# Edge loop of a graph network: the one register load per turn on TensorE moved from the twelfth step to the sixth

## The chip, the core and the metric

The kernel runs on one core of one Trainium2 chip. The metric is the device time of one execution in microseconds, the median over several runs.

## What is computed

Three message-passing layers over a graph with 3125 nodes, 100,000 edges taken in both directions, 128 node features and 16 edge features, then a residual and a layer norm. The core of the reference:

```python
for l in range(3):
    e_in = concat([h_prev[s2], h_prev[d2], ef2])          # gather two nodes per edge
    msg  = leaky_relu(e_in @ We1[l]) @ We2[l]
    red  = segment_sum(msg, d2, num_segments=N)           # scatter-add to nodes
    out  = leaky_relu(concat([h_prev, red]) @ Wn1[l]) @ Wn2[l]
    h_prev = out + h_prev
return layernorm(x + out)
```

## The kernel before

A preparation phase (up to about 1670 us) sorts the edges by the pair of node blocks that they join, so that a tile of 128 edges touches one low and one high block of 128 nodes. In each layer TensorE first multiplies the nodes by the weights (tables t_hi and t_lo, a high and a low half in float16), and then runs the edge loop over all tiles.

The edge loop is a hardware loop with 26 turns in each of the three layers, 78 in all. A turn is unrolled into 12 steps (STEPS = 12; the texts number them q = 0 to 11), a step takes three tiles (STEP = 3). On TensorE one step is, in program order:

- tile 0: `features` (L1089, a matmul into the sums bank, gath6) and four gathers (L1096) that pick table rows by a one-hot matrix gsel;
- tile 1: the same into gath, after a wait for x_set;
- tile 2: the same into gath, with a wait for mlo_set ahead of the gathers;
- sums: 12 matmuls (L1151) that add the messages of three steps ago (LAG = 3) to the node sums, after a wait for gath6_free.

ScalarE copies the gathered values out of the two PSUM places, clears the one in sums (L591) and makes a float16 copy (L597); VectorE applies the leaky ReLU (L806) and makes the low half (L875). In layer 0 VectorE also builds the one-hot matrices (L892 and L810), which are kept in HBM for layers 1 and 2.

Which blocks a tile touches is known at run time only. Each step has one 32-bit word that holds the six block numbers of its three tiles. The words lie in the SBUF row map_row, and TensorE's sequencer loads 15 of them (WORDS = STEPS + LAG: the 12 of the turn and the 3 before it, for the sums) into registers with one TENSOR_LOAD per turn, in `load_words` (L1038). `places` (its register work is put down to L1069 for the gathers and to L1077 for the sums) takes the fields out of a word. A field that was already taken out of the same copy of the words is reused: at steps 3 to 11 the sums of step q use fields that the gathers of step q - 3 took out in the same turn; at steps 0 to 2 they have to be taken out anew, from the words of the turn before. The register work appears in listings of the program as ISA rows and in the trace as FUSED_REGOPS on TensorE's sequencer; the engine named PEldq is that sequencer.

Of the kernel before, what the change touches and what calls it, by code (L numbers as in the profile page):

```python
# [32 lines left out]
STEPS = 12  # L33
LAG = 3
# [26 lines left out]
BANKS = -(-NODES // BANK)  # L61
AHEAD = 1
WORDS = STEPS + LAG
BLOCK_BITS = 5
assert NB <= 1 << BLOCK_BITS and STEP * 2 * BLOCK_BITS < 32
SLOPE = 0.01
# [14 lines left out]
def build(nc, x, src, dst, ef, We1, We2, Wn1, Wn2, c_iota, c_part, c_tri, c_ident, c_tiles, c_steps, c_mask, out):  # L81
# [9 lines left out]
    with ExitStack() as ctx:  # L91
        def sb(name, shape, dt):
            return ctx.enter_context(nc.sbuf_tensor(name, shape, dt))
# [76 lines left out]
        map_row = sb("map_row", [1, MAP_ROW], I32)  # L170
# [158 lines left out]
        def live_counts(engine):  # L329

            _, v = nc.values_load_multi_w_load_instructions(
                map_row[0:1, MAPW * P:MAPW * P + 2], engines=(engine,), min_val=1, max_val=TURNS,
                skip_runtime_bounds_check_because="counted among the turns and batches; the first always counts")
            return v
# [4 lines left out]
        def upto(p):  # L339

            return DMA * (p // 2 + 1)
# [278 lines left out]
        def _(dve):  # L620
            steps = [0]

            def then(ins):

                steps[0] += 1
                ins.then_inc(dve_seq, 1)
                dve.wait_ge(dve_seq, steps[0])
# [141 lines left out]
            for i in range(STEP):  # L769
                for s in range(2):  # L770
                    up = (2 * i + s) * BLOCK_BITS - 7
                    then(dve.tensor_scalar(tile_i[:, :, i, s], tile_i[:, :, i, s], abs(up), None,
# [170 lines left out]
        def _(pe):  # L943
# [43 lines left out]
            live_n, live_p = live_counts(mybir.EngineType.PE)  # L987
            words = [pe.alloc_register(f"word_{k}") for k in range(WORDS)]

# [22 lines left out]
            with pe.Fori(0, L) as l:  # L1012
# [23 lines left out]
                def load_words(first):  # L1036

                    pe.reg_load(words, map_row[0:1, ds(first, WORDS)])  # L1038

                load_words(0)  # L1040
                with nc.Fori(0, TURNS, engines=(mybir.EngineType.PE,), hint_back_edge=True) as it:
                    with pe.If(it < live_n):
                        word_of = [pe.snap(r) for r in words]
                        step0 = pe.snap(l * live_n * STEPS + it * STEPS)
                        turn = pe.snap((l * live_n + it) * PER_TURN)

                        def places(t):

                            q, i = divmod(t, STEP)
                            word, nodes = word_of[q + LAG], []  # L1050
                            for k in (2 * i, 2 * i + 1):
                                field = word // (1 << k * BLOCK_BITS) if k else word
                                if k + 1 < 2 * STEP:
                                    field = field - word // (1 << (k + 1) * BLOCK_BITS) * (1 << BLOCK_BITS)
                                nodes.append(nc.s_assert_within(
                                    field * P, 0, (NB - 1) * P,
                                    skip_runtime_bounds_check_because="a word holds the blocks of three tiles"))
                            return nodes

                        def rows(t, node0, plane):  # L1060

                            return t[:, plane * NODES:(plane + 2) * NODES].rearrange("p (k n) -> p k n", k=2)[:, :, ds(node0, P)]

                        def gather_rows(t):

                            lo, hi = places(t)
                            at = rows(t_hi, lo, 0), rows(t_lo, lo, 0), rows(t_hi, hi, 1), rows(t_lo, hi, 1)
                            for ap in at:
                                pe.lower_ap(ap)  # L1069
                            return at  # L1070

                        def sum_places(t):

                            lo, hi = places(t)
                            at = sums[:, ds(lo, P)], sums[:, ds(hi, P)]
                            for ap in at:
                                pe.lower_ap(ap)  # L1077
                            return at

                        def at_least(value):  # L1080

                            v = pe.snap(value)
                            pe.lower_val(v)
                            return v

                        def features(uv, t, h, fresh):

                            tc = t % PART
                            pe.matmul(uv, fchunk[:, h, tc * P:(tc + 1) * P], wst[:, :, :].rearrange("p s f -> p (s f)"),  # L1089
                                      start=fresh, stop=False, skip_group_check=True)  # L1090

                        def gather(uv, at, t, h, n):

                            tc = t % PART
                            s = n // 2
                            return pe.matmul(uv, gsel[:, h, (2 * tc + s) * P:(2 * tc + s + 1) * P], at[n], start=False,  # L1096
                                             stop=n == 3, skip_group_check=True)

                        for q in range(STEPS):
                            p = q // PART_STEPS  # L1100
                            h = p % 2
                            t = STEP * q
                            first = q % PART_STEPS == 0
                            uv6, uv7 = gath6, (gath[:, 0:2 * D], gath[:, 2 * D:4 * D])


                            rows0 = gather_rows(t)
                            if first:
                                part_in = at_least(turn + upto(p))
                            x_free = at_least(step0 + (q + AHEAD))  # L1110
                            if first:
                                pe.wait_ge(fchunk_in[h], part_in)
                            features(uv6, t, h, False)
                            if first:
                                pe.wait_ge(gsel_set[h], part_in)
                            for n in range(4):
                                last = gather(uv6, rows0, t, h, n)
                            last.then_inc(gath6_done, 1)


                            rows1 = gather_rows(t + 1)
                            pe.wait_ge(x_set, x_free)
                            features(uv7[0], t + 1, h, True)
                            for n in range(4):
                                gather(uv7[0], rows1, t + 1, h, n)


                            rows2 = gather_rows(t + 2)
                            free6 = at_least(step0 + (q + 1))
                            lo_in = at_least(step0 + (q + LO_AHEAD - LAG + 2))  # L1130
                            if first:
                                pe.wait_ge(ssel_set[1 - h], part_in)
                            features(uv7[1], t + 2, h, True)
                            pe.wait_ge(mlo_set, lo_in)
                            for n in range(4):
                                last = gather(uv7[1], rows2, t + 2, h, n)
                            last.then_inc(gath7_done, 1)


                            place = (q - LAG) % RING  # L1140
                            sum_at = {t + i - STEP * LAG: sum_places(t + i - STEP * LAG) for i in range(STEP)}
                            if q == STEPS - 1:
                                load_words((it + 1) * STEPS)
                            pe.wait_ge(gath6_free, free6)
                            for i in range(STEP):
                                at_lo, at_hi = sum_at[t + i - STEP * LAG]
                                ts = (t + i - STEP * LAG) % SLOTS
                                for s, out_n in ((1, at_hi), (0, at_lo)):
                                    w0 = i * 2 * D + (1 - s) * D
                                    for m in (m_hi, m_lo):  # L1150
                                        last = pe.matmul(out_n, m[:, place, w0:w0 + D], ssel[:, ts, s, :], start=False,  # L1151
                                                         stop=False, skip_group_check=True)
                            last.then_inc(sum_done, 1)
# [69 lines left out]
```

## Time and profile before

| what | value |
|---|---|
| median of 3 runs | 4555.39 us (4554.65 to 4555.74) |
| the profiled execution's own time | 4540.66 us |
| its span, first to last instruction | 4538.9 us |
| TensorE matmul busy | 3134.0 us, 69% |
| VectorE busy | 2927.2 us, 64% |
| ScalarE busy | 2092.5 us, 46% |
| TensorE's granted clock, mean over the span | 0.806 |

The shares are means over stages with different limits; the change concerns the edge loop alone, which fills three stretches of the span. "Idle before" is time in which an engine had nothing to run, with the releaser that ended it; "issue" as a releaser means that nothing in the trace was being waited for, so that the engine's own sequencer had not yet handed the instruction over.

### The profile page before, as it was taken

How to read it: one execution, taken by the hardware profiler on the slowest of the kernel's cores; microseconds unless marked ns; L12 is line 12 of the kernel's file. 1: busy time of each engine (PE TensorE's matmuls, PEld its weight loads, DVE VectorE, ACT ScalarE, POOL GpSimd, SP SyncE). 2: the span in 40 equal slices, each digit the busy share in tenths (PEclk: the TensorE clock that was granted, in tenths of full speed). 3: DMA queues.
4: the chain of work that ended last, by engine and by line, in shares of the span. 5: the costliest groups of instructions: out<-in, count | busy, mean ns of one | idle time of the engine just before them, and what ended most of it. 6: DMA issues, size and time to landing. Idle time of an engine off the chain costs nothing.

```text
span 4538.9 us, 95215 instructions
## 1 busy us (share of the span) xinstructions
PE 3134.0 (69%) x28957; PEld 2255.1 (50%) x28958; DVE 2927.2 (64%) x7075; ACT 2092.5 (46%) x4052; POOL 780.5 (17%) x826
## 2 busy tenths in 40 slices
PE   3443443443442558888888879898888788988886
PEld 2111111111110556666666657777777577767774
DVE  7444444444443369999999966666666566666665
ACT  0000000000000346666666667777777677777774
POOL 0455555555555100000000000000000000000000
PEclk6555555555555779999999989999999899999998
DMA  6000000000000646666565624444444244444443
GB/s 176 4 5 5 5 5 5 5 5 5 5 5 5 147 123 212 207 213 209 207 215 204 214 102 162 162 154 163 153 159 157 86 164 152 164 152 159 157 155 112
DMA packets 191495, 533.07 MB, mean 117 GB/s; under 512 B 34359, under 2 KB 71958, under 8 KB 189430
## 3 DMA queue, kind: packets, MB, share of 16 engines
q1 hardware_dynamic: 163926, 517.51, 34.1%
q0 software_dynamic: 27552, 15.37, 1.8%
q8 instruction: 6, 0.10, 0.0%
q14 instruction: 11, 0.09, 0.0%
HBM read 375.40 MB, written 157.52 MB: 117 GB/s over the span
## 4 chain that ended last, share of the span: by engine, by line
PE 46%; DVE 10%; issue 9%; DMA 2%; ACT 1%; POOL 0%; DVEq 0%; SPq 0%; ACTq 0%; POOLq 0%
PE gath L1096 16%; PE sums L1151 12%; PE sums L1096 8%; PE gath L1089 5%; DVE loop_buf L875 3%; DVE loop_buf L892 2%; DVE big L806 2%; PE sums L1089 2%; DMA recc<-records 2%; PE sums L1001 1%; DVE gsel L810 1%; PE sums L1159 0%; PE sums L1021 0%; PE sums L1160 0%; PE sums L1165 0%
## 5 line engine op out<-in xcount | busy, mean ns | idle before, releaser
L806 DVE SCALAR_TENSOR_TENSOR big<-big 128x768 f32<-128x768 f32 (+1 forms) x957 | 907.7, 949 | 676.4 <-ACT big L593 635.0
L1096 PE MATMUL gath<-t_hi,gsel 128*128 x3744 | 944.9, 278 | 0.0
L1096 PE MATMUL gath<-t_lo,gsel 128*128 x3744 | 944.3, 278 | 0.0
L1151 PE MATMUL sums<-loop_buf 128*128 128x128 f16 x11232 | 793.7, 221 | 202.6 <-issue 202.0
L875 DVE TENSOR_TENSOR loop_buf<-big,loop_buf 128x768 f16<-128x768 f32 x936 | 889.7, 951 | 0.0
L507 POOL DMA_INDIRECT records<-rec,rowi x784 | 754.7, 963 | 630.7 <-DVE rec L747 391.2
L984 PE MATMUL sums<-t_lo,tri 128*128 128x326 f16 x784 | 345.5, 454 | 714.0 <-issue 480.2
L1151 PEld LDWEIGHTS sums<-loop_buf 128*128 128x128 f16 x11232 | 680.7, 99 | 311.0 <-issue 156.8
L725 DVE SCALAR_TENSOR_TENSOR gsel<-sums,t_lo 128x326 f32<-128x326 f32 x784 | 367.3, 496 | 724.0 <-remote 536.6
L597 ACT ACTIVATE loop_buf<-big 128x768 f16<-128x768 f32 x936 | 782.0, 836 | 1.9
L593 ACT ACTIVATE big<-gath 128x512 f32<-128x512 f32 x936 | 559.6, 598 | 356.8 <-PE gath L1096 356.8
L545 ACT ACTIVATE rec<-big,sc_ef 128x224 f16 x56 | 27.0, 482 | 1356.0 <-DMA records<-rec,rowi 1239.2
L984 PEld LDWEIGHTS sums<-t_lo,tri 128*128 128x128 f16 x784 | 81.8, 104 | 1068.0 <-issue 598.4
L588 ACT ACTIVATE big<-sums 128x256 f32<-128x256 f32 x936 | 355.4, 380 | 422.8 <-PE sums L1096 421.1
L1089 PE MATMUL gath<-wst,fchunk 128*128 128x256 f16 x1872 | 527.1, 282 | 0.6
L1096 PE MATMUL sums<-t_hi,gsel 128*128 x1872 | 468.7, 277 | 22.9 <-DVE gsel L810 22.9
L1096 PE MATMUL sums<-t_lo,gsel 128*128 x1872 | 469.4, 277 | 0.0
L1096 PEld LDWEIGHTS gath<-t_lo,gsel 128*128 128x128 f16 x3744 | 374.1, 100 | 50.6
L1096 PEld LDWEIGHTS gath<-t_hi,gsel 128*128 128x128 f16 x3744 | 374.5, 100 | 31.3
L1089 PE MATMUL sums<-wst,fchunk 128*128 128x256 f16 x936 | 259.6, 277 | 171.2 <-issue 141.0
L591 ACT ACTIVATE sums<-iota 128x256 f32<-128x256 f16 x936 | 362.9, 388 | 29.6
L527 POOL PARTITION_ALL_REDUCE mxa<-mx x3 | 1.1, 358 | 1961.0 <-DVE mx L827 1961.0
(156 smaller groups left out, 2632.1 us busy)
## 6 DMA issues: line engine op xcount, KB each, us to landing
gsel<-gsel_d SPq DMA_DIRECT2D x208, 576.0 KB, 3.9
loop_buf<-ssel_d SPq DMA_DIRECT2D x208, 576.0 KB, 5.1
numb<-nums_d SPq DMA_DIRECT2D x106, 576.0 KB, 4.6
gsel_d<-gsel SPq DMA_DIRECT2D x104, 576.0 KB, 5.5
ssel_d<-loop_buf SPq DMA_DIRECT2D x104, 576.0 KB, 6.5
fchunk<-feat_d SPq DMA_DIRECT2D x313, 144.0 KB, 2.9
records<-rec,rowi POOLq DMA_INDIRECT x784
recc<-records POOLq DMA_DIRECT2D x30, 272.0 KB, 5.1
```

The costliest lines, as they stand in the source:

```text
L507: pool.indirect_dma_start(out=records[:, :], out_offset=bass.IndirectOffsetOnAxis(ap=rowi[:, h, g:g + 1].bitcast(U32), axis=0), in_=rec[:, ...
L588: act.activation(msg[:, place, 0:2 * D], gath6, ACT.Copy).then_inc(x6_set, 1)
L591: act.activation(gath6, iota[:, 0:2 * D], ACT.Copy, scale=0.0).then_inc(gath6_free, 1)
L593: act.activation(msg[:, place, 2 * D:MSG], gath[:, :], ACT.Copy).then_inc(x_set, 1)
L597: act.activation(m_hi[:, (q - 1) % RING, :], msg[:, (q - 1) % RING, :], ACT.Copy)\
L725: dve.scalar_tensor_tensor(scrap[c], bank(1 + c)[:, 0:BUCKETS], 1.0, onehot[:, c * GROUP + g, :], ALU.mult, ALU.mult, accum_out=slot_f[:, ...
L806: return dve.scalar_tensor_tensor(m, m, SLOPE, m, ALU.mult, ALU.max)
L875: dve.tensor_tensor(m_lo[:, place, :], msg[:, place, :], m_hi[:, place, :], ALU.subtract)\
L984: pe.matmul(bank(1 + c)[:, 0:BUCKETS], tri[:, 1, :], onehot[:, c * GROUP + g, :], start=False, stop=False, skip_group_check=True)
L1089: pe.matmul(uv, fchunk[:, h, tc * P:(tc + 1) * P], wst[:, :, :].rearrange("p s f -> p (s f)"), start=fresh, stop=False, skip_group_check=True)
L1096: return pe.matmul(uv, gsel[:, h, (2 * tc + s) * P:(2 * tc + s + 1) * P], at[n], start=False, stop=n == 3, skip_group_check=True)
L1151: last = pe.matmul(out_n, m[:, place, w0:w0 + D], ssel[:, ts, s, :], start=False, stop=False, skip_group_check=True)
```

## The change

The load of the words is issued at q = 5 (LOAD_AT = 6, the sixth step) of the same turn instead of at q = 11. It loads 15 words that start at the turn's seventh place: the first nine serve steps 6 to 11 of this turn and the sums of steps 6 to 8, and the same registers serve steps 0 to 5 of the next turn. The words are copied into fresh registers a second time after the load (`word_of = [pe.snap(r) ...]`). Before the loop, only the nine words that the first half turn needs are loaded.

```diff
+LOAD_AT = STEPS // 2
...
-                load_words(0)
+                pe.reg_load(words[LOAD_AT:], map_row[0:1, 0:WORDS - LOAD_AT])
                 with nc.Fori(0, TURNS, engines=(mybir.EngineType.PE,), hint_back_edge=True) as it:
                     with pe.If(it < live_n):
                         word_of = [pe.snap(r) for r in words]
+                        now = 0
...
                             q, i = divmod(t, STEP)
-                            word, nodes = word_of[q + LAG], []
+                            word, nodes = word_of[q + LAG + (LOAD_AT if now < LOAD_AT else -LOAD_AT)], []
...
                         for q in range(STEPS):
+                            now = q
...
-                            if q == STEPS - 1:
-                                load_words((it + 1) * STEPS)
+                            if q == LOAD_AT - 1:
+                                load_words(it * STEPS + LOAD_AT)
+                                word_of = [pe.snap(r) for r in words]
                             pe.wait_ge(gath6_free, free6)
```

The instruction order on TensorE at the end of step 5 and the start of step 6, before (sums<-loop_buf are the sums, sums<-wst,fchunk the first features of a step):

```order
L1077 ISA x2
L1151 MATMUL sums<-loop_buf 128x128 x12
L1069 ISA x3
L1089 MATMUL sums<-wst,fchunk 128x256
L1096 MATMUL sums<-t_hi,gsel 128x256
```

The same place in the changed kernel (its lines stand one to four further down):

```order
L1079 ISA x2
L1039 ISA
L1039 TENSOR_LOAD map_row
L1147 ISA
L1155 MATMUL sums<-loop_buf 128x128 x12
L1071 ISA x3
L1091 MATMUL sums<-wst,fchunk 128x256
```

The load now stands ahead of the sums of step 5, with one further row of register work, the second copy of the words (L1147).

The register work between tile 2 and the sums of step 6 on TensorE, before:

```order
L1069 ISA x2
L1083 REGISTER_ALU
L1089 MATMUL gath<-wst,fchunk 128x256
L1096 MATMUL gath<-t_hi,gsel 128x256
L1096 MATMUL gath<-t_lo,gsel 128x256
L1096 MATMUL gath<-t_hi,gsel 128x256
L1096 MATMUL gath<-t_lo,gsel 128x256
L1077 ISA x2
L1151 MATMUL sums<-loop_buf 128x128 x12
```

And in the changed kernel:

```order
L1071 ISA x2
L1085 REGISTER_ALU
L1091 MATMUL gath<-wst,fchunk 128x256
L1098 MATMUL gath<-t_hi,gsel 128x256
L1098 MATMUL gath<-t_lo,gsel 128x256
L1098 MATMUL gath<-t_hi,gsel 128x256
L1098 MATMUL gath<-t_lo,gsel 128x256
L1079 ISA x6
L1155 MATMUL sums<-loop_buf 128x128 x12
```

Where two rows of register work stood ahead of the sums, six stand now. The same holds at steps 7 and 8; at steps 0, 1 and 2 there are six both before and after, and at the other six steps two.

The end of the turn on TensorE, before:

```order
L1077 ISA x2
L1038 ISA
L1038 TENSOR_LOAD map_row
L1151 MATMUL sums<-loop_buf 128x128 x12
L1042 UNCONDITIONAL_BRANCH
L1041 REGISTER_ALU
L1041 COMPARE_AND_BRANCH
```

And in the changed kernel:

```order
L1079 ISA x2
L1155 MATMUL sums<-loop_buf 128x128 x12
L1043 UNCONDITIONAL_BRANCH
L1042 REGISTER_ALU
L1042 COMPARE_AND_BRANCH
```

The load and its address work are gone from there; the sums and the branches stay.

## Rows read from the trace of the kernel before

**Rows 1.** Edge loop by layer: us, then busy (instructions) of each engine, clock, DMA
```profile
core 0: us, PE busy (x) PEld busy (x) DVE busy (x) ACT busy (x) POOL busy (x), PEclk, DMA share, GB/s
1672.13:2618.14 946.01, 794.61 (x8397) 638.39 (x8398) 923.42 (x2602) 641.19 (x1243) 0.00 (x0) 0.98 0.60 208
2677.00:3546.00 869.00, 772.49 (x8397) 632.95 (x8398) 566.38 (x620) 629.45 (x1243) 0.00 (x0) 0.98 0.46 157
3605.04:4475.08 870.04, 774.80 (x8398) 635.39 (x8399) 566.27 (x620) 629.78 (x1243) 0.00 (x0) 0.97 0.45 157
```

**Rows 2.** Waits of TensorE from 2700 to 3540 us (layer 1): total, times, longest
```profile
PE sums L1151 <- issue: 66.0, 82, 1.4
PE sums L1089 <- issue: 29.8, 25, 1.3
```

**Rows 3.** Timeline of TensorE over one turn of layer 1: start, us, instruction, idle before
```profile
3080.99 0.28 PE L1089 MATMUL sums<-wst,fchunk 128*128 128x256 f16 x1 [1.19 <-issue]
...
3084.21 0.27 PE L1089 MATMUL sums<-wst,fchunk 128*128 128x256 f16 x1
...
3087.41 0.28 PE L1089 MATMUL sums<-wst,fchunk 128*128 128x256 f16 x1
...
3089.91 0.84 PE L1151 MATMUL sums<-loop_buf 128*128 128x128 f16 x12 [0.63 <-issue]
3090.59 0.27 PE L1089 MATMUL sums<-wst,fchunk 128*128 128x256 f16 x1
...
3108.70 0.83 PE L1151 MATMUL sums<-loop_buf 128*128 128x128 f16 x12
3109.38 0.27 PE L1089 MATMUL sums<-wst,fchunk 128*128 128x256 f16 x1
...
3112.53 0.84 PE L1151 MATMUL sums<-loop_buf 128*128 128x128 f16 x12 [1.29 <-issue]
...
3114.55 0.28 PE L1089 MATMUL sums<-wst,fchunk 128*128 128x256 f16 x1 [1.19 <-issue]
```

**Rows 4.** The sequencer's L1077 in step 2, then in step 3: ns min/median/max, first and last start
```profile
L1077 PEldq FUSED_REGOPS  x6: 51/184/188, 3088.6 to 3089.8; - x6
...
L1077 PEldq FUSED_REGOPS  x2: 74/79/84, 3091.8 to 3091.9; - x2
```

**Rows 5.** The sequencer at the end of that turn: the load, branches, copy of the words
```profile
L1038 PEldq TENSOR_LOAD <-map_row x1: 1585/1585/1585, 3110.9 to 3110.9; - x1
...
L1041 PEldq COMPARE_BRANCH  x1: 249/249/249, 3112.7 to 3112.7; - x1
...
L1043 PEldq FUSED_REGOPS  x2: 195/214/232, 3113.3 to 3113.6; - x2
```

**Rows 6.** TensorE's sequencer loads two words once (L331)
```profile
L331 PEldq TENSOR_LOAD <-map_row x1: 723/723/723, 1457.7 to 1457.7; - x1
```

**Rows 7.** Two neighbouring turns of layer 1, the first 4.4 us of each, a turn of layer 0
```profile
3047.42:3080.99 33.57, 30.47 (x325) 25.15 (x325) 21.93 (x24) 24.35 (x48) 0.00 (x0) 0.95 0.46 158
3080.99:3114.56 33.57, 29.24 (x325) 23.82 (x325) 21.93 (x24) 24.35 (x48) 0.00 (x0) 1.00 0.46 158
3047.00:3051.40 4.40, 3.98 (x28) 3.15 (x29) 0.34 (x1) 1.74 (x4) 0.00 (x0) 0.61 0.80 286
3080.60:3085.00 4.40, 3.38 (x34) 2.43 (x35) 1.44 (x2) 2.15 (x5) 0.00 (x0) 1.00 0.81 263
2111.71:2148.02 36.31, 30.04 (x324) 24.03 (x325) 35.84 (x102) 24.79 (x48) 0.00 (x0) 1.00 0.64 211
```

**Rows 8.** Timeline of TensorE in that turn of layer 0: waits for others
```profile
2129.20 0.28 PE L1096 MATMUL sums<-t_hi,gsel 128*128 x1 [0.50 <-DVE gsel L810]
...
2137.39 0.28 PE L1089 MATMUL sums<-wst,fchunk 128*128 128x256 f16 x1 [0.95 <-DMA fchunk<-feat_d]
```

**Rows 9.** DMA issues by transfer: count, KB, median us from issue to landing
```profile
fchunk<-feat_d SPq DMA_DIRECT2D x313, 144.0 KB, 2.9
```

## The prediction

> **What bounds the kernel now.** I first cut the span into its stretches. The edge loops of the three layers take 946, 869 and 870 us [rows 1], 2685 of 4539; the change touches nothing else. In layers 1 and 2 TensorE is busy 89% of the loop and VectorE 65%. So next I asked what ends TensorE's idle time there: the list of waits names "issue" alone, 66.0 us ahead of the sums and 29.8 us ahead of a turn's first features [rows 2]. The 25 waits of that second row are one for each turn but the first.
>
> Then I laid one turn out along TensorE's timeline, by the start of each step's first matmul [rows 3]. Three kinds of step appear:
> - steps 0, 1, 2: 3084.21 - 3080.99 = 3.22 us, then 3.20 and 3.18 us, with 0.63 us idle ahead of the sums;
> - steps 3 to 10, eight of them: (3109.38 - 3090.59) / 8 = 2.35 us, without idle time;
> - step 11: 3114.55 - 3109.38 = 5.17 us, with 1.29 us idle ahead of the sums and 1.19 us ahead of the next turn.
>
> Together 33.57 us. What distinguishes steps 0 to 2 is the sequencer's own work: six FUSED_REGOPS at L1077 between tile 2 and the sums, the first starting at 3088.6 and the last at 3089.8, right before the sums start at 3089.91; in step 3 there are two, of 74 and 84 ns [rows 3, 4]. So in these three steps TensorE waits for its sequencer's arithmetic, and in the eight others that arithmetic just fits behind the matmuls. Step 11 has the TENSOR_LOAD of 1.585 us, then the loop's branches and the copy of the words, from 3112.7 on [rows 5].
>
> One thing that looks important isn't. In some turns the granted clock falls to its lower level of 1.2 GHz after the two stalls of step 11: 0.61 on average over the first 4.4 us of one turn, against 1.00 in the next. Yet both turns take 33.57 us [rows 7]: the slow matmuls fill the gaps that the sequencer leaves in steps 0 to 2. If two stalls that no longer stand side by side keep the clock up, that is worth nothing.
>
> In layer 0 VectorE is busy 35.84 of a turn's 36.31 us [rows 7], and TensorE waits for it and for a transfer in steps 6 and 9 [rows 8]. That stage is bound by VectorE.
>
> **The change, part by part (layers 1 and 2, one turn).**
>
> *The load leaves step 11.* In a plain step the sums start 3108.70 as against a next step at 3109.38, 0.68 us earlier, so 2.35 - 0.68 = 1.67 us after the step's start. In step 11 they start at 3112.53 - 3109.38 = 3.15 us, 1.48 late [rows 3]. Of the step's excess of 5.17 - 2.35 = 2.82 us the load thus makes 1.48, and the back edge the other 1.34. Step 11 becomes 2.35 + 1.34 = 3.69 us. The back edge itself does not get cheaper: its branches and register rows start once the sums have been handed over, and the sums cover 0.68 us of them, with or without a load ahead. The register rows at the head stay five in number.
>
> *The load enters step 5.* Step 5 is a plain step like 11, so the sequencer is as little ahead of the array there: the load costs 1.48 us again. Behind it comes the second copy of words (L1147), a row that the trace does not have there; the nearest are the two copy rows at L1043, 195 and 232 ns [rows 5]. I take 0.20 plus some 0.05 to the next instruction, 0.25 us; its bounds are 0, if something else held the sums longer, and 0.3. Step 5 becomes 2.35 + 1.48 + 0.25 = 4.08 us.
>
> *The reuse is cut at step 6.* The fields that the gathers of steps 3 to 5 took out come from the old copy, so the sums of steps 6, 7 and 8 have to take theirs out of the new one: six rows for two, twelve more per turn. From row 4 four more of them take (3089.8 - 3088.6) + 0.05 for the six, less 0.1 + 0.08 for the two, some 1.07 us, of which a plain step hides some 0.2 in its slack; measured as a whole, 3.18 - 2.35 = 0.83 us per step [rows 3, 4]. After the load of step 5 the sequencer has no lead either, as after the one of step 11, so each of the three steps should pay in full: 2.49 us. What hides such work today is the length of the array's own 2.35 us; that cover is already used up. Bounds: 0, if the sequencer had a lead, and 1.07 x 3 = 3.2 us.
>
> The new turn: 9.60 (steps 0 to 2) + 4.70 (3, 4) + 4.08 (5) + 9.54 (6 to 8) + 4.70 (9, 10) + 3.69 (11) = 36.31 us against 33.57, +2.74. Times 52 turns: +142 us.
>
> *Layer 0.* TensorE's own turn would be the same 36.3 us; VectorE's is 35.84 busy. Its waits for VectorE and the transfer in steps 6 and 9 (0.50 and 0.95 us) should mostly go, since VectorE catches up while TensorE stalls in steps 5 to 8. The turns there average 946.0 / 26 = 36.4 us now. Two engines that both need 36 us and lean on each other take a bit more than either: I take 36.7, +0.3 per turn, +8 us over 26. Bounds: -0.1 (36.3) and +2.74 (nothing absorbed), so -3 to +71 us.
>
> *Before the loop.* Nine words instead of 15. Two words take 0.723 us and fifteen 1.585 [rows 5, 6], so 0.066 us a word, -0.4 us in each layer, -1 us in all.
>
> Sum: 142 + 8 - 1 = +149 us on the profiled execution's own 4540.7, so 4690. The median of the runs stands 14.7 us above that execution; on its level this is 4555.4 + 149 = 4704 us. A difference within 0.2%, some 9 us, is about what a measurement of this kernel can't tell from no change.
>
> **A rule against this.** The rows say that the sequencer has almost no lead: a load of 1.585 us leaves the array idle for 1.29 us [rows 3, 5]. The Trainium skill, "Advanced Engine Details and Errata", section Engine Queue Depths, gives TensorE a queue of 64 instructions. A step has 27 matmuls and as many weight loads, 54, so by that rule the sequencer could be a whole step of 2.35 us ahead and hide both the load and the extra rows; in this trace it is not. By the rule the time would be rival B's 4568 or, with the load hidden too, rival C's 4440; by the rows it is 4704.
>
> **Rivals.**
> - *A: layer 0 pays too.* If its stalls add up instead of overlapping, with half or all of 2.74 x 26 = 71 us, the time is 4732 to 4767. For: VectorE has only 0.47 us to spare per turn, and may now miss its inputs in step 5 as well. Against: today it absorbs step 11's 2.82 us. 17 in 100.
> - *B: the twelve extra rows are hidden.* The mechanism would be a lead of the sequencer in steps 6 to 8. Then only the copy of words is left, 0.25 x 52 = 13 us: 4568; half hidden, 4636. For: steps 3 to 10 hide all of their register rows [rows 3]. Against: steps 0 to 2, with the very rows that steps 6 to 8 get, are idle each time. 5 in 100.
> - *C: faster, the load is covered.* If in mid turn TensorE had some 2 us queued when the load begins, it would cost nothing there, and also give the sequencer time for B: -1.48 x 78 = -115, so 4440. It decides if the queued work exceeds 1.585 us; with any less, and with B's rows in force, the result is slower. Against: the steps before step 11 look exactly like those before step 5, and there 1.29 us stay exposed. 3 in 100.
> - *D: the loop's longer code.* The body grows by 12 rows of register work. If the branch back then had to fetch its target, each turn would pay a transfer, for which the nearest row is the 2.9 us of fchunk [rows 9]: 78 x 2.9 = +226, so 4930. The branch takes 249 ns now, in which nothing is fetched [rows 5]. That a taken branch outside the prefetched window stalls on a fetch is the rule of the Trainium skill, "Runtime: NRT & Kernel Launch", section Instruction fetch mechanics; no run here shows such a stall. 3 in 100.
>
> **How the numbers follow.** The forecast has 72 in 100. Its own range comes from 2.2 to 3.0 us per turn over 52 turns (114 to 156) and -3 to +36 in layer 0: 4666 to 4747. B's and C's cases lie below, the upper part of A and D above. I give 4670 to 4748. Faster: C, 0.03. Same: B at its far end, 0.02. Slower: the rest, 0.95.
>
> **What would show it.** In the profile after: a turn of layers 1 and 2 near 36.3 us; steps 6, 7 and 8 near 3.18 us with some 0.63 us idle <-issue ahead of the sums; step 5 near 4.1 with an idle of about 1.5 ahead of its sums; step 11 near 3.7 with some 1.2 us ahead of the next turn, unchanged; a TENSOR_LOAD of 1.58 us as before; 48 rows at the sums' register line per turn where 36 were; layer 0's turns at 36.3 to 37; fewer or no stretches at the lower clock. The prediction is wrong if steps 6 to 8 stay at 2.35 (B), if step 5 shows no idle time (C), or if layer 0's turns come near 39 (A).

## The result and the profile after

The changed kernel takes 4873.28 us (median of 4 runs, 4869.23 to 4878.48), the kernel before 4555.02 us (4552.97 to 4555.74). The ratio is 1.070 with an interval of 1.068 to 1.072: +318 us, where +149 was forecast, and outside the range of 4670 to 4748.

The edge loop of the changed kernel by layer, the whole of each; us, busy times of the engines, clock and DMA as in [rows 1]:

```profile
1688.66:2695.82 1007.16, 820.18 (x8398) 658.72 (x8399) 922.75 (x2602) 638.67 (x1243) 0.00 (x0) 0.94 0.58 195
2752.61:3754.44 1001.83, 817.21 (x8398) 656.35 (x8399) 566.23 (x620) 638.98 (x1243) 0.00 (x0) 0.94 0.40 136
3810.97:4812.50 1001.53, 815.83 (x8398) 655.35 (x8399) 566.23 (x620) 638.58 (x1243) 0.00 (x0) 0.94 0.40 136
```

Against [rows 1] the loops are 61, 133 and 131 us longer, 325 us of the 336 by which the profiled spans differ. The first 25 turns of layers 0 and 1, from the first features of the first turn to those of the 26th, before:

```profile
1672.13:2586.68 914.55, 765.93 (x8101) 615.04 (x8101) 892.91 (x2517) 619.36 (x1200) 0.00 (x0) 0.98 0.61 208
2676.99:3517.64 840.65, 745.99 (x8100) 611.09 (x8101) 548.10 (x600) 607.96 (x1200) 0.00 (x0) 0.97 0.45 156
```

And in the changed kernel:

```profile
1688.66:2660.71 972.05, 791.36 (x8101) 635.72 (x8101) 890.62 (x2510) 616.85 (x1200) 0.00 (x0) 0.94 0.58 195
2752.61:3719.62 967.01, 788.69 (x8100) 633.29 (x8101) 547.17 (x600) 617.16 (x1200) 0.00 (x0) 0.94 0.40 136
```

A turn of layer 0 thus went from 914.55 / 25 = 36.58 us to 38.88, one of layer 1 from 33.63 to 38.68. The timeline of TensorE over one turn of layer 1, the counterpart of [rows 3]:

```profile
3148.83 0.27 PE L1091 MATMUL sums<-wst,fchunk 128*128 128x256 f16 x1
...
3153.51 0.27 PE L1091 MATMUL sums<-wst,fchunk 128*128 128x256 f16 x1
...
3158.92 1.46 PE L1155 MATMUL sums<-loop_buf 128*128 128x128 f16 x12 [3.56 <-issue]
3160.17 0.42 PE L1091 MATMUL sums<-wst,fchunk 128*128 128x256 f16 x1
...
3163.46 0.27 PE L1091 MATMUL sums<-wst,fchunk 128*128 128x256 f16 x1
...
3166.20 0.27 PE L1091 MATMUL sums<-wst,fchunk 128*128 128x256 f16 x1
...
3168.67 0.84 PE L1155 MATMUL sums<-loop_buf 128*128 128x128 f16 x12 [0.60 <-issue]
3169.35 0.27 PE L1091 MATMUL sums<-wst,fchunk 128*128 128x256 f16 x1
...
3174.05 0.27 PE L1091 MATMUL sums<-wst,fchunk 128*128 128x256 f16 x1
...
3177.60 0.28 PE L1091 MATMUL sums<-wst,fchunk 128*128 128x256 f16 x1 [1.02 <-issue]
```

Steps 3 and 4 still take (3153.51 - 3148.83) / 2 = 2.34 us, steps 6 to 8 take (3169.35 - 3160.17) / 3 = 3.06 us, step 11 3.55 us. The surprise is step 5: 3160.17 - 3153.51 = 6.66 us, with 3.56 us idle ahead of the sums. Its reason stands in the rows of the load's two lines, in the loop (L1039, 15 words) and ahead of it (L1041, 9 words); ns min/median/max, first and last start:

```profile
L1039 PEldq TENSOR_LOAD <-map_row x78: 3570/3576/3602, 1705.3 to 4793.5; - x78
...
L1041 PEldq TENSOR_LOAD <-map_row x3: 868/873/885, 1686.1 to 3808.4; - x3
```

The same instruction with the same 15 words took 1.585 us before [rows 5] and takes 3.576 us now, in each of the 78 turns within 1%. The nine words ahead of the loop take 0.873 us, so it isn't the program's loads as such. In the loop the 15 words start at word 12 x turn + 6, that is, at byte 48 x turn + 24 of the row: never at a multiple of 16 bytes. Before, they started at byte 48 x (turn + 1), always at one.

Two theories: **A**, the start of the load sets its cost; **P**, the place in the turn does, by what else uses the memory there. (They are not the prediction's rival A.)

### The profile page after: what moved, and what is told of

The parts are those of the page before. It is cut to its first block, busy times and chain, and to the rows that moved or that the text cites. A ratio compares the mean times of both kernels' runs of the same rounds, so it can differ in the third digit from the quotient of the medians.

```text
span 4874.9 us, 96229 instructions
## 1 busy us (share of the span) xinstructions
PE 3249.1 (67%) x28957; PEld 2322.8 (48%) x28958; DVE 2924.8 (60%) x7075; ACT 2108.3 (43%) x4052; POOL 778.5 (16%) x826
## 4 chain that ended last, share of the span: by engine, by line
PE 47%; issue 12%; DMA 5%; DVE 3%; SPq 1%; ACT 1%; POOL 0%; DVEq 0%; ACTq 0%; POOLq 0%
PE gath L1098 16%; PE sums L1155 13%; PE sums L1098 8%; PE gath L1091 5%; DMA fchunk<-feat_d 3%; PE sums L1091 2%; DMA recc<-records 2%; PE sums L1002 1%; DVE loop_buf L876 1%; PE sums L1163 0%; PE sums L1022 0%; DVE gsel L811 0%; DVE big L807 0%; PE sums L1164 0%; DVE loop_buf L893 0%
## 5 line engine op out<-in xcount | busy, mean ns | idle before, releaser
L1155 PE MATMUL sums<-loop_buf 128*128 128x128 f16 x11232 | 834.8, 227 | 479.5 <-issue 479.0
L1155 PEld LDWEIGHTS sums<-loop_buf 128*128 128x128 f16 x11232 | 706.3, 102 | 627.4 <-issue 386.9
L1098 PE MATMUL gath<-t_hi,gsel 128*128 x3744 | 964.0, 283 | 0.0
L1098 PE MATMUL gath<-t_lo,gsel 128*128 x3744 | 960.5, 282 | 0.0
L1098 PE MATMUL sums<-t_hi,gsel 128*128 x1872 | 488.4, 286 | 0.0
L1098 PE MATMUL sums<-t_lo,gsel 128*128 x1872 | 488.2, 286 | 0.0
```

## The experiments

Runs are compared with the kernel before beside them on the same chip. For the first eight that kernel took 4192 to 4193 us, and no trace of it was kept there. The run with a sixteenth word, which is the same up to its loop, has its first load at 1322.4 us instead of 1668.8, some 346 us earlier. From the first load to the end that leaves 4192.2 - 1322.4 = 2870 us, as against 4540.7 - 1668.8 = 2872 us: the turns are of the same length, by this difference. Why the preparation is shorter there stays open. The lengths of turns below are those of 25 turns of layer 1, unless layer 0 is named.

### The row two words further, in the changed kernel

ROW0 = 2 moves the whole row of words, so that the load of step 5 starts at byte 48 x turn + 32.

```diff
+ROW0 = 2
...
-            sp.dma_start(map_row[:, 0:MAPW * P], ...)
+            sp.dma_start(map_row[:, ROW0:ROW0 + MAPW * P], ...)
...
-                    pe.reg_load(words, map_row[0:1, ds(first, WORDS)])
+                    pe.reg_load(words, map_row[0:1, ds(first + ROW0, WORDS)])
```

The load ahead of the loop and the two words behind the row move along with it.

> The changed kernel with the row of words placed two words (8 bytes) further into its buffer, so that the load of step 5 starts at 48 x turn + 32 bytes instead of + 24, and nothing else changes. Theory A (the load is slow because its first word isn't at a multiple of 16 bytes): the load takes 1.59 us again instead of 3.58, a turn about 36.6 us, the time 4873 - 78 x 2.0 = 4717 us. Theory P (the load is slow because of what else goes on in the middle of a turn): 3.58 us and 4873 us as before.

Measured: 4319.09 us against 4192.23, ratio 1.030 (1.027 to 1.033), +127 us, where theory A gave +162, with a turn of 36.6 us. Its load in the loop, and the nine words ahead of it, which now are the ones that start 8 bytes off:

```profile
L1040 PEldq TENSOR_LOAD <-map_row x78: 1572/1578/1601, 1343.3 to 4237.5; - x78
...
L1042 PEldq TENSOR_LOAD <-map_row x3: 2186/2187/2191, 1323.5 to 3313.1; - x3
```

The load is as before, and the nine words have gone from 0.87 to 2.19 us. The place in the turn is the same, so P falls as the cause of the 3.58 us. Its 25 turns of layer 0 and of layer 1, at 36.28 and 36.14 us each:

```profile
1327.33:2234.27 906.94, 751.88 (x8100) 594.56 (x8101) 892.90 (x2514) 619.50 (x1200) 0.00 (x0) 1.00 0.61 209
2323.82:3227.35 903.53, 750.06 (x8100) 594.79 (x8101) 547.18 (x600) 619.39 (x1200) 0.00 (x0) 1.00 0.42 145
```

Its timeline of one turn of layer 1:

```profile
2807.91 0.27 PE L1092 MATMUL sums<-wst,fchunk 128*128 128x256 f16 x1
...
2811.31 0.84 PE L1156 MATMUL sums<-loop_buf 128*128 128x128 f16 x12 [1.55 <-issue]
2812.02 0.28 PE L1092 MATMUL sums<-wst,fchunk 128*128 128x256 f16 x1
...
2814.53 0.84 PE L1156 MATMUL sums<-loop_buf 128*128 128x128 f16 x12 [0.62 <-issue]
2815.21 0.27 PE L1092 MATMUL sums<-wst,fchunk 128*128 128x256 f16 x1
...
2821.53 0.28 PE L1092 MATMUL sums<-wst,fchunk 128*128 128x256 f16 x1
...
2826.24 0.27 PE L1092 MATMUL sums<-wst,fchunk 128*128 128x256 f16 x1
...
2829.80 0.28 PE L1092 MATMUL sums<-wst,fchunk 128*128 128x256 f16 x1 [0.99 <-issue]
```

This is the turn that the prediction drew: step 5 takes 4.11 us (4.08 predicted), steps 6 to 8 (2821.53 - 2812.02) / 3 = 3.17 (3.18), step 11 3.56 (3.69), the turn 36.14 (36.31).

### The row further by two words, and by one, in the kernel before

The same edit in the kernel before, with ROW0 = 2 and ROW0 = 1.

> The kernel before with the row of words placed two words further, so that its load of step 11 starts 8 bytes off a multiple of 16. Theory A: the load takes 3.58 us where it took 1.59, the time is 4555 + 78 x 2.0 = 4711 us. Theory P: nothing changes, 4555 us.

Measured: 4384.23 us against 4192.23, ratio 1.045 (1.042 to 1.049), +192 us, where theory A gave +156. Its load:

```profile
L1039 PEldq TENSOR_LOAD <-map_row x81: 3565/3571/3584, 1324.4 to 4321.5; - x81
```

The turns are 35.86 us in layer 1 and 39.29 in layer 0, over 33.63 and 36.58 in the kernel before: +2.2 and +2.7 us, more than the 1.99 us of the load itself. This is the counterpart of the run above: 192 us for a load that starts 8 bytes off, here as there (318 - 127 = 191).

> The kernel before with the row of words one word (4 bytes) further. If only a start at a multiple of 16 bytes is fetched four words at a time, the load takes 3.58 us, the same as two words off, and a turn of layers 1 and 2 lasts 33.6 + 2.0 + some 0.2 = 35.9 us, +2.2 us x 78 = +175 us over the kernel before. If it were a matter of 8-byte pairs (7 pairs and one word where the row is two words off), one word off would be slower still than two words off, 4 us or more.

Measured, in one run: 4388.56 us against 4192.90. Its load:

```profile
L1039 PEldq TENSOR_LOAD <-map_row x81: 3565/3571/3583, 1324.6 to 4322.1; - x81
```

It takes 3.571 us as well. One word off costs the same as two; pairs of words play no part.

### The number of words

WORDS = STEPS + LAG + 1 in the kernel before, a sixteenth word that nothing uses:

> The kernel before with 16 words per load instead of 15; the sixteenth is not used. If words are fetched one by one at some 0.07 to 0.22 us each, the load takes 1.65 to 1.8 us and the time is 4560 to 4572 us. If four words that start at a multiple of 16 bytes are one fetch and the rest single ones (15 = 3 fetches + 3 singles, 16 = 4 fetches), at the 0.22 us per fetch that the loads of 15 words suggest (3.58 - 1.59 over 9 fetches), the load takes 1.15 us and the time is 4555 - 78 x 0.44 = 4521 us.

Measured: 4163.47 us against 4192.23, ratio 0.993 (0.990 to 0.996). One word more makes the load faster:

```profile
L1038 PEldq TENSOR_LOAD <-map_row x81: 1102/1106/1122, 1322.4 to 4099.3; - x81
```

Then 12 words from a multiple of 16 bytes (by ROW0 = 1), with the three older ones carried over in registers; ahead of the loop the three and the twelve are loaded apart:

```diff
-                    pe.reg_load(words, map_row[0:1, ds(first, WORDS)])
+                    for k in range(LAG):
+                        pe.reg_mov(words[k], word_of[STEPS + k])
+                    pe.reg_load(words[LAG:], map_row[0:1, ds(first + LAG + ROW0, STEPS)])
```

> The kernel before, but a turn loads only its 12 new words, starting at a multiple of 16 bytes (the row stands one word further), and the three words of the turn before are copied from registers. By one fetch of 0.23 us for four words the load takes three fetches, 0.87 us as the load of nine words did, 0.7 us less than before, less some 0.15 us for the copies: -0.55 x 78 = -43 us. If a load's cost is in its number of words whatever their place, 12 words take 1.585 x 12 / 15 = 1.27 us: -0.17 x 78 = -13 us.

Measured: 4147.50 us against 4192.90, ratio 0.990 (0.987 to 0.993), -45 us. The load takes 0.852 us.

All sizes of load in the study, by words and by the byte at which they start modulo 16, with the number of fetches if four words that start at a multiple of 16 are one fetch and any others single ones:

| words | start | fetches | us |
|---|---|---|---|
| 2 | 0 | 2 | 0.72 |
| 3 | 4 | 3 | 0.78 |
| 9 | 0 | 3 | 0.87 |
| 12 | 0 | 3 | 0.85 |
| 7 | 0 | 4 | 1.08 |
| 16 | 0 | 4 | 1.11 |
| 11 | 0 | 5 | 1.32 |
| 15 | 0 | 6 | 1.58 |
| 9 | 8 | 9 | 2.19 |
| 10 | 4 | 10 | 2.42 |
| 15 | 4 or 8 | 15 | 3.57 |

The ten words are those ahead of the loop in the run with LOAD_AT = 7 below, the three those ahead of the loop with 12 words:

```profile
L1042 PEldq TENSOR_LOAD <-map_row x3: 2415/2418/2424, 1687.6 to 3799.8; - x3
```

```profile
L1043 PEldq TENSOR_LOAD <-map_row x3: 782/782/788, 1320.9 to 3220.6; - x3
```

The times follow the fetches, not the words: from 3 fetches to 15 it is (3.57 - 0.85) / 12 = 0.227 us each, and three single words cost 0.78 us where twelve from a multiple of 16 bytes cost 0.85. The ten words contain four that lie at a multiple of 16 bytes, and by the table these too were fetched singly: what counts is the start of the load. That the load really is split so is a reading of these rows; the times are measured.

The Trainium skill, "Runtime: NRT & Kernel Launch", section Instruction fetch mechanics, gives a TENSOR_LOAD some 200 ns per register, "even for bulk", and means the loads that the runtime inserts. The loads from SBUF here come near it where they start off a multiple of 16 bytes (3.57 / 15 = 0.238 us); the others do not, with 1.106 / 16 = 0.069 us.

### Other places in the turn

The changed kernel with LOAD_AT = 4, 7 and 8, each with a start at a multiple of 16 bytes (for 7 by ROW0 = 1) and with the number of words ahead of the loop to match.

> The changed kernel with the load one and a half parts into the turn, at the fourth step (q = 3) instead of the sixth, so that it starts at 48 x turn + 16 bytes. Theory A: 1.59 us, a turn about 36.6 us, the time about 4717 us, with six rows of register work ahead of the sums at steps 4, 5 and 6. Theory P: it is still in the middle of a turn, so about 3.6 us and 4870 us.

Measured: 4442.23 us against 4192.23, ratio 1.059 (1.056 to 1.062), 123 us more than with the load in step 5. The load in layer 0, then in layers 1 and 2:

```profile
L1039 PEldq TENSOR_LOAD <-map_row x26: 4151/4292/4445, 1334.7 to 2359.4; - x26
...
L1039 PEldq TENSOR_LOAD <-map_row x52: 1572/1582/1600, 2452.6 to 4355.7; - x52
```

In layers 1 and 2 theory A is right. In layer 0 something else adds 2.7 us. In one turn the two transfers that read the one-hot matrices out of SBUF are issued by the sync engine at 1743.4 and 1743.9, and the load starts at 1744.6:

```profile
L442 SPq DMA_DIRECT2D gsel_d<-gsel x1: 338/338/338, 1743.4 to 1743.4; - x1
...
L445 SPq DMA_DIRECT2D ssel_d<-loop_buf x1: 332/332/332, 1743.9 to 1743.9; - x1
...
L1039 PEldq TENSOR_LOAD <-map_row x1: 4209/4209/4209, 1744.6 to 1744.6; - x1
```

The load ends at 1744.6 + 4.2 = 1748.8, and the first transfer lands 5.5 us after its issue, at 1748.9. Layers 1 and 2 have transfers of the same size in the other direction, into SBUF, and no delay. The turns of layer 0 are longer by more than the load: the next load starts at 1785.5, so a turn takes 40.9 us, 4.6 more than the 36.28 of the run with the load in step 5. Why it is 4.6 and not 2.7 stays open.

> The changed kernel with the load at the seventh step (q = 6) and the row one word further, so that it starts at a multiple of 16 bytes. In the run with the load at q = 3 it took 1.58 us in layers 1 and 2 but 4.15 to 4.45 us in layer 0, where the sync engine issues the two transfers that read the one-hot matrices out of SBUF (gsel_d<-gsel, ssel_d<-loop_buf) some 1.2 us ahead of it. Theory T (these transfers hold the load up): q = 6 has the same place in the three-step pattern, so again about 4.3 us in layer 0 and 1.58 us in layers 1 and 2. Theory Q (something special to the fourth step, such as the first part's end): 1.58 us in all layers.

> The same with the load at the eighth step (q = 7), its start a multiple of 16 bytes without a shift. Theory T: the load begins some 3 to 4 us after the two transfers were issued, which take 5.5 and 6.5 us to land, so it is held up for the rest of them: between 2 and 4 us in layer 0. If VectorE's work on the same buffers in layer 0 held the load up, it would do so at each step: about 4.3 us. Layers 1 and 2: 1.58 us.

Measured, one run each, against 4558.77 us: 4803.28 us with the load in step 6, 4737.89 with it in step 7. The loads of layer 0, in step 6, then in step 7:

```profile
L1040 PEldq TENSOR_LOAD <-map_row x25: 3927/4741/4858, 1712.6 to 2694.4; - x25
```

```profile
L1039 PEldq TENSOR_LOAD <-map_row x26: 2727/2782/2906, 1718.7 to 2675.9; - x26
```

In layers 1 and 2 both take 1.58 to 1.59 us. So the steps with q = 3 and 6 meet the transfers from their start, and q = 7 meets their second half. With q = 5 the load of one turn of layer 0 starts 6.4 us after the first transfer was issued, which by then has landed, and takes 1.58 us. In one turn of each run the held load ends within 0.3 us of the landing of the first transfer: 1748.8 and 1748.9 with q = 3, 2043.5 and 2043.4 with q = 6, 2027.9 and 2027.6 with q = 7. The second transfer lands over a microsecond later each time.

Theory T, as expected there, thus holds at each place that was tried. VectorE's work does not explain it: VectorE is as good as always busy in layer 0, and with q = 5 no load is held up. Nor does the amount of traffic. With q = 7 the load of one turn of layer 1 falls into the middle of the two transfers into SBUF, with the 16 DMA engines fully busy at 409 GB/s, and takes 1.575 us:

```profile
L1039 PEldq TENSOR_LOAD <-map_row x1: 1575/1575/1575, 3018.7 to 3018.7; - x1
```

```profile
3018.70:3020.30 1.60, 0.31 (x3) 0.03 (x1) 1.08 (x2) 1.28 (x3) 0.00 (x0) 1.00 1.01 409
```

One rival was not separated by a run of its own: layer 0 also has a transfer of 576 KB into SBUF (numb<-nums_d), issued 0.5 us ahead of the two.

### The reuse kept

The changed kernel with ROW0 = 2, in which a tile of the first half turn takes its word from the copy at the head of the turn (now head_words) also after the load:

```diff
-word, nodes = word_of[q + LAG + (LOAD_AT if now < LOAD_AT else -LOAD_AT)], []
+word, nodes = head_words[q + LAG + LOAD_AT] if q < LOAD_AT else word_of[q + LAG - LOAD_AT], []
```

> The changed kernel with the row two words further (load at a multiple of 16 bytes) and with the reuse mended: the sums of steps 6 to 8 take the blocks of steps 3 to 5 from the words copied at the head of the turn, so two rows of register work stand ahead of them instead of six. If the twelve extra rows cost 0.83 us per step, a turn falls from the 36.14 us of the run with the shifted row to 33.65 us, and the time is the kernel before plus 0.25 x 78 = +20 us at most. If they cost nothing, the turn stays at 36.14 us.

Measured: 4180.87 us against 4192.90, ratio 0.9968 (0.9954 to 0.9981), -12 us. Layer 0 and layer 1, 25 turns each:

```profile
1324.93:2220.44 895.51, 752.06 (x8100) 601.98 (x8101) 887.63 (x2510) 616.79 (x1200) 0.00 (x0) 1.00 0.63 212
2309.50:3152.35 842.85, 733.07 (x8100) 598.40 (x8101) 547.56 (x600) 611.38 (x1200) 0.00 (x0) 1.00 0.46 156
```

The turn of layer 1 falls from 36.14 to 33.71 us, 2.43 for the twelve rows. Over the whole kernel they cost 127 + 12 = 139 us, the difference of two runs that were each compared with the kernel before. With both mended, the moved load is a small gain: layers 1 and 2 stay 0.1 us per turn above the kernel before, layer 0 is at 35.82 us per turn below its 36.58.

### A faster version

Two kernels with all that the runs suggest. In both a word is copied when it is first used (`if k not in of: of[k] = pe.snap(words[k])`), which takes the copies off the head of the turn. That edit, with 16 words, in the kernel before:

> The kernel before with 16 words per load (load 1.11 us) and with each word copied when it is first used instead of all at the head of the turn. If the register rows at the head are exposed in full, the two rows of copies, 0.43 us and their 0.12 us of issue, less one short row, come off every turn: turn 33.23 - 0.45 = 32.8 us, and steps 3 to 8, which get the copies, stay at 2.35 us if they have slack for one more short row, or grow by up to 0.1 us each. In all -0.9 x 78 = -70 us against the kernel before; if the slack isn't there, some -20 us.

Measured: 4142.40 us against 4192.90, ratio 0.989 (0.986 to 0.992), -50 us, where -70 or, without slack, -20 was expected; a turn takes 33.05 us, 0.18 less than with 16 words alone (33.23), and not 0.45. Step 11 falls from 4.82 to 4.44 us in one turn of each, but the other eleven steps, which now hold the copies (213 ns and more each), grow by some 0.2 us together.

> The changed kernel with all that the runs so far mended: load in the sixth step from a multiple of 16 bytes, 16 words, reuse kept across the load, each word copied at its first use. From the 33.71 us turn of layers 1 and 2 in the mended kernel with 15 words: the load 0.47 less, the copy at step 5 (0.25) and the copies at the head (0.2 to 0.3) gone: 32.75 us. Layer 0, which was 0.5 us per turn below the kernel before with the load in mid turn, about 34.9 to 35.3 us. In all -(0.85 x 52 + 1.4 x 26) = -80 us, ratio 0.981.

> The kernel before with 12 words per load from a multiple of 16 bytes, three words carried over in registers, and each word copied at its first use. From the run with late copies and 16 words (turn 33.05 us): the load 0.26 us less, the three carried words 0.1 to 0.15 us more: 32.9 us. Layer 0 about 35.7 us. In all some -60 us, ratio 0.986: behind the kernel with the load in mid turn if separating the two stalls helps layer 0, ahead of it if it doesn't.

Measured against 4558.77 us: the load in step 5, 16 words, reuse kept: 4505.91 us, ratio 0.988 (0.986 to 0.990); the load in step 11, 12 words: 4508.69 us, ratio 0.989 (0.987 to 0.990). That is -53 and -50 us, where -80 and -60 were expected. Their turns are 33.07 and 33.04 us in layer 1, where 32.75 and 32.9 were expected, and 35.81 and 35.83 us in layer 0, where 34.9 to 35.3 was expected of the first: VectorE is busy for 887 of 895 us there, so nothing that TensorE's sequencer saves can show below that. The two places of the load come out the same.

## Why the prediction was wrong

- **What bounds the kernel, and the turn's three kinds of step: right.** Steps 0 to 4 are unchanged, and TensorE waits for its sequencer at every place named. The sequencer's lead is as short as the rows said, also in mid turn: a load of 3.576 us leaves the array idle for 3.56, one of 1.578 for 1.55.
- **The load enters step 5 for 1.48 us again: this step failed.** It took the duration of one TENSOR_LOAD for that of another with the same number of words, and so had step 5 at 4.08 us, where it takes 6.66. The new start is 8 bytes off a multiple of 16, and the load takes 3.576 us. Shown both ways, by mending it in the changed kernel (191 us) and by breaking it in the kernel before (192 us). The bounds of that term held only the row of copies; none was put on the load. The small term *Before the loop* had the same fault: at 0.066 us a word, by the difference of two loads [rows 5, 6], the nine words would have taken 1.19 us, and they take 0.87.
- **Of those 191 us, 1.99 x 78 = 155 are the longer load itself.** The rest goes with the lower clock, as far as two turns show. The profile after has a granted clock of 0.94 in the loops, against 0.98, 0.98 and 0.97 [rows 1], and turns differ by it:

```profile
3139.27:3177.60 38.33, 31.06 (x324) 25.07 (x325) 21.96 (x25) 24.67 (x48) 0.00 (x0) 0.96 0.41 139
3177.60:3216.90 39.30, 32.19 (x325) 26.05 (x325) 21.96 (x25) 24.69 (x48) 0.00 (x0) 0.91 0.39 135
```

  In both turns the array is idle for 3.56 us ahead of the sums of step 5 and then runs at the lower level, 1.2 GHz: the twelve sums take 1.46 us instead of 0.84, a matmul of the next step 0.42 instead of 0.27. In the turn shown above that lasts for somewhat over half of step 6. In the next it lasts through all of it:

```profile
3197.35 1.46 PE L1155 MATMUL sums<-loop_buf 128*128 128x128 f16 x12 [3.56 <-issue]
3198.60 0.42 PE L1091 MATMUL sums<-wst,fchunk 128*128 128x256 f16 x1
...
3203.08 0.31 PE L1091 MATMUL sums<-wst,fchunk 128*128 128x256 f16 x1
```

  Step 6 takes 4.48 us there, and 3.29 in the turn before it. The whole turns are 38.33 and 39.30 us, 2.19 and 3.16 above the 36.14 with the mended start, of which the load itself is 2.00. That the clock is worth nothing was right for the two short stalls of the kernel before [rows 7] and wrong behind this long one. That it makes up all of the rest over all 78 turns was not shown.
- **The reuse is cut, 0.83 us at each of three steps: right.** 2.43 us per turn measured, 2.49 forecast. A turn has 48 rows at the sums' register line, as forecast, and 36 again with the reuse kept.
- **The load leaves step 11 for 1.48, the back edge keeps 1.34: right.** Step 11 is at 3.55 us, 3.69 forecast.
- **Layer 0 absorbs its share: right with the start mended, its size and sign not.** There its turn is 36.28 us against 36.58 before, 0.3 less, where 0.3 more was forecast and 0.1 less was the bound: some -8 us instead of +8. Why it gets shorter was not shown. With the long load TensorE needs 38.7 us, as in layer 1, which is over what VectorE needs, and layer 0 pays 61 us.
- **The rivals.** B and C fell: the rows and the load are both exposed. D did not happen, the back edge is no longer than before. A's size, +61 us in layer 0, was nearly reached, but by the long load; with the start mended its mechanism does not show.

With the start mended, the sum of +149 us stands against a measured +127, with each step of the turn within 0.15 us of its forecast. What took the time out of the range was the size of one term, the load in step 5: taken at 1.48 us per turn, it came to 2.0 us more by the load alone, and to 191 us over the whole kernel, more than the whole sum.

## What to carry to other kernels

When an instruction is moved, its operand's address moves too: look at what its start is a multiple of before taking its duration from the old row. Let a register load start at a multiple of 16 bytes and read whole groups of four words, even if some go unused; put it where no large transfer out of the same memory is in flight. And where values are cached by the copy that they came from, a new copy in mid loop cuts the reuse: keep the old one for what was begun with it.

## What the runs showed of the hardware

- A TensorE register load from SBUF took 1.11 us for 16 words and 1.58 for 15 from a multiple of 16 bytes, 3.57 us for 15 words off one. All its times fit some 0.23 us per fetch, with four words per fetch from such a start and one word per fetch otherwise.
- The same load takes longer while transfers that read SBUF are in flight, up to the landing of the first: 4.3 and 4.7 us instead of 1.58 right behind their issue, 2.8 us some 3 us later. Beside transfers that write SBUF, at 409 GB/s, it took 1.575 us.
- In two neighbouring turns TensorE ran at its lower level, 1.2 GHz, behind 3.56 us without a matmul. In the run with the mended start, with 1.55 us there, the granted clock is 1.00 over the 25 turns.
